# A convolution kernel's head in another order: middle kernel row by taps on ScalarE's queue, mixes interleaved, one variance moved

## The reference

```python
def _gn(v, G=32, eps=1e-05):            # group norm, no affine part
    ...
    return ((g - m) / jnp.sqrt(s + eps)).reshape(v.shape)

def _L0_conv_ref(x, w_route, b_route, w_experts, bn_gamma, bn_beta, bn_mean, bn_var):
    pooled = jnp.mean(x, axis=(2, 3))
    routing = jax.nn.sigmoid(pooled @ w_route.T + b_route)
    ...                                  # y: 3x3 convolution of x with 4 expert kernels
    out = jnp.einsum('beohw,be->bohw', y, routing)
    inv = bn_gamma / jnp.sqrt(bn_var + BN_EPS)
    out = out * inv[None, :, None, None] + (bn_beta - bn_mean * inv)[None, :, None, None]
    return jax.nn.silu(out)

def _L1_conv_ref(x, W):
    return conv3x3(x, jnp.sign(W))       # 128 to 128 channels, padding 1

x = x + _L0_conv_ref(_gn(x), ...)
x = x + _L1_conv_ref(_gn(x), L1_conv_W)
```

## Time and profile before

| | us |
|---|---|
| median of 3 runs | 275.54 |
| lowest and highest | 274.31, 275.61 |
| the profiled execution's own time | 278.07 |
| its span in the trace | 276.3 |
| mean granted clock of TensorE | 0.986 |

### The profile page before, as it was taken

How to read it: one execution, slowest core, us unless ns; L and a number is a source line. 1 busy time by engine, 2 the same in 40 slices (tenths; PEclk the granted TensorE clock), 3 DMA queues, 4 the chain that set the end, 5 groups by cost and what they waited for, 6 DMA issues and landing times.

```text
span 276.3 us, 4108 instructions
## 1 busy us (share of the span) xinstructions
PE 267.7 (97%) x1334; PEld 184.3 (67%) x1334; DVE 256.0 (93%) x466; ACT 219.4 (79%) x449; POOL 54.1 (20%) x62
## 2 busy tenths in 40 slices
PE   8899989999999999999999999999999999999993
PEld 8654755848576675948676685858677685948562
DVE  5779979999999999999999999999999999995984
ACT  2478889897979889897989989798989986835860
POOL 2002011311203141312203141312304141210120
PEclk9689999999999999999999999999999999999999
DMA  6999944372555536263455536263554536182407
GB/s 213 394 357 295 304 161 80 84 133 85 95 136 76 142 50 116 85 116 106 76 152 78 128 59 119 81 112 114 78 152 72 120 61 132 76 141 90 76 2 152
DMA packets 11254, 35.20 MB, mean 127 GB/s; under 512 B 1249, under 2 KB 3425, under 8 KB 11233
## 3 DMA queue, kind: packets, MB, share of 16 engines
q0 software_dynamic: 4176, 15.21, 32.7%
q1 hardware_dynamic: 6768, 19.47, 19.3%
q10 hardware_dynamic: 288, 0.26, 0.3%
HBM read 11.34 MB, written 16.25 MB: 100 GB/s over the span
## 4 chain that ended last, share of the span: by engine, by line
PE 90%; DVE 2%; ACT 2%; DMA 2%; issue 1%; SPq 0%; POOL 0%; DVEq 0%; ACTq 0%
PE pc L565 40%; PE pa L530 14%; PE pb L530 14%; PE pe_ L530 12%; PE pd L520 6%; DMA X<-x 2%; PE pd L460 1%; PE ps L500 1%; ACT y L885 1%; ACT junk_mid L737 1%; PE ps L504 1%; PE pa L602 0%; POOL rstd L419 0%; PE pb L602 0%; DVE X L1331 0%
## 5 line engine op out<-in xcount | busy, mean ns | idle before, releaser
L1119 DVE SCALAR_TENSOR_TENSOR U<-we,route,U 128x1152 f32<-128x1152 f32 x45 | 63.7, 1416 | 0.6
L565 PE MATMUL pc<-hi,ws 128*128 128x496 f16 (+3 forms) x270 | 59.8, 375 | 0.8 <-ACT hi L894 0.8
L565 PE MATMUL pc<-lo,ws 128*128 128x496 f16 (+3 forms) x270 | 59.7, 375 | 0.0
L419 POOL TENSOR_TENSOR rstd<-ve,nhalf 128x2 f32<-128x2 f32 (+1 forms) x19 | 26.4, 1392 | 137.8 <-ACT ve L809 113.1
L565 PEld LDWEIGHTS pc<-hi,ws 128*128 128x128 f16 x270 | 26.4, 98 | 30.3 <-issue 1.2
L565 PEld LDWEIGHTS pc<-lo,ws 128*128 128x128 f16 x270 | 26.5, 102 | 27.8
L530 PE MATMUL pa<-V,UM 128*128 128x256 f32 (+1 forms) x180 | 41.7, 381 | 0.0
L530 PE MATMUL pb<-V,UM 128*128 128x256 f32 (+1 forms) x180 | 40.7, 376 | 0.1
L530 PE MATMUL pe_<-V,U 128*128 128x256 f32 (+1 forms) x180 | 40.6, 375 | 0.0
L530 PEld LDWEIGHTS pb<-V,UM 128*128 128x128 f32 x180 | 34.1, 190 | 5.4 <-issue 0.6
L530 PEld LDWEIGHTS pe_<-V,U 128*128 128x128 f32 x180 | 34.1, 190 | 3.8
(11 more groups left out here) (161 smaller groups left out, 399.4 us busy)
## 6 DMA issues: line engine op xcount, KB each, us to landing
X<-x SPq DMA_DIRECT2D x15, 512.0 KB, 5.2
out<-X SPq DMA_DIRECT2D x15, 512.0 KB, 2.6
out<-ev POOLq DMA_DIRECT2D x15, 512.0 KB, 5.4
X<-y POOLq DMA_DIRECT2D x14, 512.0 KB, 4.5
we<-w_experts SPq DMA_DIRECT2D x3, 768.0 KB, 9.2
ws_raw<-w_sign SPq DMA_DIRECT2D x1, 576.0 KB, 12.1
out<-X SPq DMA_DIRECT2D x1, 384.0 KB, 2.5
X<-x ACTq DMA_DIRECT2D x2, 128.0 KB, 2.9
```

What stands on the lines that cost most here:

```text
L419: g.tensor_tensor(rstd[:, c, a:b], ve[:, c, a:b], nhalf[:, a:b], ALU.pow).then_inc(rstd_ready, 1)
L565: mm = mm_(rows[:, r0 - first // W:r1 - first // W, c0:c1], ws[:, tap * C:(tap + 1) * C], plane((hi, lo)[part], i)[:, r0 + ky - 1:r1 + ky ...
L1119: v.scalar_tensor_tensor(out=flat(U[i % RING][:]), in0=flat(we[:, e, :, :]), scalar=route[:, i, e:e + 1], in1=flat(U[i % RING][:]), op0=AL ...
```

## The change

- The middle kernel row is no longer loaded on SP's queue. ACT's queue loads it behind its two quarters of image 0 as three loads, one for each tap, middle tap first, with a semaphore for each.
- DVE computes `pooled` of image 0 before it waits for image 1. The top rows of `xn[0]` are now written by ACT, and the scaled copy of expert 0 for part 0 by DVE (`first_copy`).
- The mixes of parts 0 to 3 are interleaved by a new `FIRST_MIX`, with the aggregate and column steps of image 1 between them; the mixes of image 1 go between its transforms.
- PE's warming products are 40, 8, 13, 20 instead of 40, 8, 15, 16, 7, and `group_mean(1)` stands behind the first half of part 0.
- ACT takes `mean_in(2)` ahead of `routing(1)`, `variance(1)` behind the copy of part 3, `copy_minus(1)` ahead of `var_mid(0)`, and `mix(2)` from before `squares(LAG)` to behind `deviation` of the first pass of the loop.
- In the loop's first pass DVE takes `mix(2, 1)` ahead of `pool_routes(3)`.

```diff
-WARM = (40, 8, 15, 16, 7)
-FIRST_MIX = tuple((p, x) for p in range(4) for x in (1, 2, 3))
+WARM = (40, 8, 13, 20)
+FIRST_MIX = ((0, 1), (0, 2), (0, 3), (1, 1), (1, 2), (2, 1), (1, 3), (2, 2), (3, 1), (2, 3), (3, 2), (3, 3))
...
-        we_loaded = [sem(f"we_loaded{g}") for g in range(K)]
+        we_loaded = [sem(f"we_loaded{g}") for g in (G0, G2)]
+        we_middle_loaded = [sem(f"we_middle_loaded{kx}") for kx in range(K)]
...
             load(1)
-            load_row(G1, 1)
             load_row(G0, 0)
...
             warm(WARM[3])
+            direct_part(0, 0, 0)
             group_mean(1)
-            warm(WARM[4])
-            direct_part(0, 0, 0)
+            direct_part(0, 0, 1)
             group_var(1)
-            direct_part(0, 0, 1)
             direct_part(0, 1, 0)
+            direct_part(0, 1, 1)
             route_logits(1)
-            direct_part(0, 1, 1)
             direct_part(0, 2, 0)
             group_mean(2)
-            direct_part(0, 2, 1, slice(0, 2))
+            direct_part(0, 2, 1)
             group_var(2)
-            direct_part(0, 2, 1, slice(2, 3))
...
             for q in (1, 3):
                 act.dma_start(quarter(q), x_quarters[0, q, :, :]).then_inc(x_quarter_loaded[q], 16)
+            for kx in KX_ORDER:
+                taps = slice(kx * C, (kx + 1) * C)
+                act.dma_start(we[:, :, G1, taps], we_v[:, 1, :, taps]).then_inc(we_middle_loaded[kx], 16)
...
             bias(0, IN)
+            normalise_rows(0, 0, H // 2 + 1, xn_top_ready)
             routing(0)
-            mix_first_part(0, 0)
             mix_first_part(0, 1)
-            deviations(1)
             normalise_rows(0, H // 2 + 1, H)
             mix_first_part(0, 2)
+            deviations(1)
+            mix_first_part(0, 3)
             variance(1)
             bias(1, IN)
             pooled_plane(1)
             normalise(1)
-            mix_first_part(0, 3)
+            mean_in(2)
             routing(1)
             mix(1)
-            mean_in(2)
...
             routing(2)
-            mix(2)
             squares(LAG)
             add_variance(LAG, IN)
+            copy_minus(1)
             var_mid(0)
             add_variance(LAG, MID)
-            copy_minus(1)
...
                 deviation(c)
+                if t == 1:
+                    mix(2)
                 bias(c, MID)
...
+            def first_copy():
+
+                dve.wait_ge(route_ready, 1)
+                dve.wait_ge(we_middle_loaded[1], 16)
+                v.tensor_scalar(kernel_part(U[0], 0), kernel_part(we[:, 0, :, :], 0), route[:, 0, 0:1], None,
+                                ALU.mult).then_inc(first_copied, 1)
...
             first_variance()
+            first_pooled()
             dve.wait_ge(x_loaded[1], 16)
             part_stats(1, 0)
-            first_pooled()
             part_stats(1, 1)
-            top_rows()
+            first_copy()
+            mix_part(0, 1)
+            mix_part(0, 2)
+            mix_part(0, 3)
             aggregate(1)
+            mix_part(1, 1)
             columns(1)
-            for part in range(2):
-                for x in (1, 2, 3):
-                    mix_part(part, x)
+            mix_part(1, 2)
             mix_part(2, 1)
+            mix_part(1, 3)
+            mix_part(2, 2)
+            mix_part(3, 1)
+            mix_part(2, 3)
             pool_routes(1)
-            mix_part(2, 2)
-            mix_part(2, 3)
+            mix_part(3, 2)
             bn_factor()
+            mix_part(3, 3)
+            all_rows(1)
             bn_scales()
-            all_rows(1)
+            inner_rows(1)
             bn_offset()
-            mix_part(3, 1)
-            inner_rows(1)
-            mix_part(3, 2)
+            mix(1, 1)
             transform_minus(1)
-            mix_part(3, 3)
+            mix(1, 2)
             transform_plus(1)
+            mix(1, 3)
             transform_ends(1)
-            mix(1, 1)
-            mix(1, 2)
-            mix(1, 3)
             pool_routes(2)
...
-                pool_routes(t + LAG - 1)
                 if t == 1:
                     mix(t + 1, 1)
+                pool_routes(t + LAG - 1)
```

More of the change, by code:

```diff
@@ L204, in build @@
         xn_top_ready = sem("xn_top_ready")
+        first_copied = sem("first_copied")
         mix_first = sem("mix_first")
@@ L275, in firsts_before @@
         def firsts_before(t):
-            return len(DIRECT_PARTS) * min(t, ND) + rank(t)
+            return (len(DIRECT_PARTS) - 1) * min(t, ND) + rank(t)
         def kernel_part(u, part):
@@ L829, in normalise, with normalise_rows @@
                 normalise_rows(i, 0, H)
-            def normalise_rows(i, first, last):
+            def normalise_rows(i, first, last, ready=xn_ready):
                 act.wait_ge(nbias_in_ready, i + 1)
@@ L834, in normalise_rows @@
                            img(i).rearrange("p (h w) -> p h w", h=H)[:, first:last, :], ACT.Identity,
-                           bias=nbias[:, i, IN:IN + 1], scale=rstd[:, i, IN:IN + 1]).then_inc(xn_ready, 1)
+                           bias=nbias[:, i, IN:IN + 1], scale=rstd[:, i, IN:IN + 1]).then_inc(ready, 1)
             def routing(i):
@@ L848, in mix @@
                     act.wait_ge(direct_ready, 2 * (i - RING + 1))
-                for g in range(K):
-                    act.wait_ge(we_loaded[g], 16)
+                for loaded in we_loaded + we_middle_loaded:
+                    act.wait_ge(loaded, 16)
                 activation(flat(U[i % RING][:]), flat(we[:, 0, :, :]), ACT.Copy,
@@ L855, in mix_first_part @@
                 act.wait_ge(route_ready, i + 1)
-                act.wait_ge(we_loaded[DIRECT_PARTS[part][0]], 16)
+                slot, taps = DIRECT_PARTS[part]
+                for loaded in [we_middle_loaded[kx] for kx in taps] if slot == G1 else [we_loaded[slot]]:
+                    act.wait_ge(loaded, 16)
                 activation(kernel_part(U[i % RING], part), kernel_part(we[:, 0, :, :], part), ACT.Copy,
@@ L1086, in first_pooled @@
                                        in1=bshare[:], op0=ALU.mult, op1=ALU.add).then_inc(pooled_ready, 1)
-            def top_rows():
-                dve.wait_ge(nbias_in_ready, 1)
-                dve.wait_ge(zeroed, 4 + RING)
-                last = H // 2 + 1
-                v.tensor_scalar(xn[0][:, 1:1 + last, :], img(0).rearrange("p (h w) -> p h w", h=H)[:, 0:last, :],
-                                rstd[:, 0, IN:IN + 1], nbias[:, 0, IN:IN + 1], ALU.mult, ALU.add) \
-                 .then_inc(xn_top_ready, 1)
+            def first_copy():
[3 more added lines that the diff above has]
+                                ALU.mult).then_inc(first_copied, 1)
             def pool_routes(c):
@@ L1102, in mix_part @@
             def mix_part(part, e):
-                if e == 1:
-                    dve.wait_ge(mix_first, part + 1)
+                if e == 1 and part == 0:
+                    dve.wait_ge(first_copied, 1)
+                elif e == 1:
+                    dve.wait_ge(mix_first, part)
                 else:
```

## The result

The changed kernel takes **281.66 us** in the median of 4 runs (280.81 to 286.07), against 275.12 for the kernel before in the same comparison (4 runs, 274.31 to 275.61). The ratio is 1.0213 [1.0163, 1.0263] (in brackets the 95% interval), so the change costs some 2%. The forecast was 274.3 with a range of 273.0 to 276.3: it missed on the other side. The profiled execution took 282.12 us with a span of 280.3; against the profiled one of before (278.07 and 276.3) that is only 4.0 us more. The medians differ by 6.5.

What follows compares the result with a forecast made beforehand. TensorE was taken to bound the kernel (busy 97%), VectorE close behind. An earlier TensorE start at slot 1, -1.4, and a later bias, +0.2, sum to -1.2: 275.54 becomes 274.3 us, range 273.0 to 276.3.

Steps and rivals of the forecast that it cites:

- (b): Loads: taps on ScalarE's queue leave the outer rows' landing at 12.3 and 14.3, bounds -0.8 and +0.7 us.
- (c): Order of the mixes: part 1's products wait for row 0, start at 14.05; TensorE would reach slot 1 at 27.85.
- the taps are starved: Rival, chance 0.15: engines alternate run by run, outer taps land about 13.7, slot 1 is late; 277.0 us.
- (f): `mix(2)` moved into the wait for rstd: bias 0.2 us late, hole before the first sign product grows by that.
- (a): Head: `pooled`, no longer behind image 1, starts at about 7.6 instead of 8.63; TensorE's idle 1.35 shrinks to 0.4.
- (d): ScalarE's chain for slot 1: GpSimd's power takes 0.55 + 0.3 us; first combination at 28.3, TensorE's start 28.4.
- (e): TensorE's start at slot 1: the later of 27.85 and 28.4, against 29.80, so 1.4 us won.
- the clock falls again: Rival, chance 0.2: TensorE idles 1.5 us after part 0's second half, then runs at half speed; 275.3 us.
- Better: Rival, chance 0.2: outer rows land 0.6 us sooner and the power is quick, gain 2.3 less 0.2; 273.4 us.

Runs made afterwards that it cites:

- the kernel that holds its rows: The changed kernel, with SP issuing rows 0 and 2 only after all three taps have landed: 280.01 us, ratio 1.0159.
- the 80 products: The changed kernel with 80 warming products between part 0's first half and `group_mean(1)`: 279.12 us, ratio 1.015.
- the execution that took 273.95: The kernel before, unchanged, profiled in another execution, the fastest of its 8: median 276.18 us, ratio 1.0023.
- the row on SP: The changed kernel with the middle row as one load of 1,536 B runs on SP's queue behind image 1: 275.95 us, ratio 1.0021.
- the taps on SP: The changed kernel with its three tap loads issued by SP behind image 1, ahead of rows 0 and 2: 276.0 us, ratio 1.0019.
- the whole row on ScalarE's queue: The changed kernel with the middle row as one load of 1,536 B runs on ScalarE's queue: 279.1 us, ratio 1.0127.

## Why the prediction was wrong

**The step that failed is (b)**, the landing of the taps. It added up bytes and time per run over the 16 engines and took the mean of -0.8 and +0.7 for what the loads do to each other. It thereby assumed that the loads arrive roughly in the order of their issue, so that the outer taps are there when ScalarE wants them: nowhere in the sum stands a wait for them, and (c) lets part 1 wait for row 0 at 12.3 alone. The two queues here did not do that. The last tap landed at 14.9, ScalarE stood 5.50 us for it, TensorE 3.52, and part 1 started at 18.73 instead of 14.05. The price per run was right: 543 runs of 512 B in the 1 us from 7 to 8 of the kernel that holds its rows is 34 on each engine, 27 ns apiece by the engines' share of 92%, against my 28. The rows came about as (b) had it or sooner, at 11.2 and 14.2 against 12.3 and 14.3. Only the taps, the one load the new order needs first, were not given a landing of their own in the forecast.

**The rival "the taps are starved" was the right mechanism**: turns run by run, three engines waiting, `columns(1)` holding TensorE, half clock behind it. Its point of decision (a landing of 13.2) was passed by 1.7. Its chance of 0.15 was too small: I kept it there because no rows showed two queues with unequal runs, which is a reason for a wide range and not for a small chance. Its price was too low as well. It gave 277.0, and 281.7 was measured. First, its own terms add up to more: 30.4 and 1.5 less 29.80, with the 0.2 of (f), is 2.3 over 275.54, which is 277.8. The 3.8 us that are left are three things. The landing was 14.9 instead of 13.7: 1.2. It left out that part 0's second half, now behind `group_mean(1)`, runs after the wait and at half clock, and the clock's fall cost 2.6 in the profile (34.43 less 33.47, and another 1.6 because with the 80 products the last tap landed at 16.5 instead of 14.9) instead of 1.5: 1.1. The rest, 1.5, is the yardstick: the own times of the two profiled executions differ by 4.05 and the medians by 6.5, which is 2.5 more, and against it stand about 0.6 by which the changed kernel's profile is shorter behind the minus points (245.9 against 246.5) and 0.4 between the 275.54 taken and the 275.12 measured.

**The yardstick** failed under (a), (d) and (e). I noted that the profiled execution was 2.5 us over the median and went on to take differences within it. But part of what I "won" was exactly what that execution had lost: image 1 landing at 8.02 (1.14 us of waiting) and 6.65 us of half clock (in windows of a tenth it is 8.9 to 15.7, 6.8 us). In the execution that took 273.95 there is neither, `pooled` starts at 7.64, and direct products at 10.53; the new order with the row on SP has 7.70 and 10.78. The forecast of 28.4 for TensorE's start at slot 1 was beaten by 1.35 us (27.05), and the old order, in its best execution, beats it by 1.95. Without the load part the change comes to 1.0021 [0.9982, 1.006], inside what can't be told from nothing.

**Point by point.** (a) `pooled` free of image 1: right as a mechanism, 8.09 with 0.74 us of waiting for GpSimd and none for the image, later than the forecast 7.6 because slot 0's own statistics came later; TensorE's idle 0.47, forecast 0.4. (c) From part 1's start to slot 1: 13.8 forecast, 13.98 in the row on SP. Right. (d) The power beside mixes of 384 columns: 0.83 us at 14.18 in the row on SP and 0.55 in the changed kernel, where VectorE mostly stood idle. I had taken 0.55 + 0.3, so right. The Trainium skill (SBUF — State Buffer, "SBUF: two separate sides") has the port locked for one instruction at a time; the 0.83 beside short mixes against 1.71 beside long ones agrees. (f) The hole grew to 0.90, 0.1 and not 0.2, and alone the part is worth nothing (0.9985 [0.9951, 1.0019]). Part right, size halved.

**The rival "the clock falls again"** was half right. With the taps on SP (profiled 277.16) the clock was low from 11.0 to 14.4, right after an idle of 1.25 us, and the minus points were 1.64 later than with the row on SP. It is a scatter of both kernels, though, and doesn't separate them. "Better" had its condition only with the middle row back on SP's queue: there the outer rows landed at 11.2 and 13.2, 1.1 us sooner than before's 12.3 and 14.3, TensorE's start came at 27.05 where this rival has 27.5, and still the time stayed at 1.0021 instead of falling by 2.1 us. What failed in it is the yardstick too.

## What to carry to other kernels

A load that is needed first should not stand with short runs on a second queue beside long runs on the first: the engines served both by the run here, so each queue's bytes go by the length of its runs, and issuing it earlier doesn't help. Put urgent loads ahead in the same queue, where 512 B runs did no harm here. And before a forecast takes a wait or a clock's fall out of a profile, ask whether that execution's own time is the median's: here a trace 2.5 us above it had up to 3.35 us in its head (29.80 against 26.45) that another execution of the same kernel did not have.

## What the runs showed of the hardware that was not expected

- Turns between two queues were one to one to within a few per cent where both had work on all engines: 183 to 180, 185 to 187, 89 to 87, 99 to 96. A tiny load is late too beside a busy second queue, though turns alone don't explain it: the parameters, 48 B on each partition, landed 3.6 us after their issue before, 4.2 in the changed kernel, and 5.8 with the whole row on ScalarE's queue.
- A load's landing is set by the one engine that is last. In the changed kernel the taps moved 187 runs from 9 to 10 but only 11 from 12 to 13 and 12 from 13 to 15, and the semaphore came at 14.9: some 2.5 us, by these counts, for a last engine's share. This is the part of the landing that no sum over 16 engines gives.
- The kernel before, unchanged, spreads from 274.26 to 279.43 in 35 executions on one chip. The longest ones have the lower mean clock, and with 13 more warming products in the head 11 of 12 executions were at 275.39 or below; the twelfth is the 397.03.
- The last store of the kernel took 2.4 us to land in one profiled execution and 3.6 in another, at the same place and size. A microsecond of difference between two single executions can lie there.
